# Attention stage: router products behind the fourth projection instead of the third, the last two turns behind the third instead of the second; first expert unit: its first low-weight pass behind the second tile's high passes

## The reference, cut to what matters

```python
h = _layernorm(x) * (1 + ca) + sa
qkva = einsum('bnd,ed->bne', rmsnorm(h), w_qkva)      # q, kv, a: 512 columns each
a = sigmoid(a);  s[t] = a[t] * s[t-1] + kv[t];  x = x + ga * q * s
h = _layernorm(x) * (1 + cb) + sb
probs = softmax(h @ Wr);  top 2 of 8 experts, capacity 160 rows for each sequence and expert
y = relu(h_e @ W1[e] + b1[e]) @ W2[e] + b2[e];  x = x + gb * (weighted sum of the two)
```

## Time and profile before

| | us |
|---|---|
| median of 3 runs | 2142.61 (2138.87 to 2143.8) |
| the profiled execution, its own time | 2142.84 |
| its span, first to last instruction | 2141.1 |
| TensorE busy | 2117.1 (99%) |
| VectorE busy | 1783.2 (83%) |
| ScalarE busy | 1062.6 (50%) |
| GpSimd busy | 368.9 (17%) |

### The profile page before, as it was taken

One profiled execution on the slowest core, in us unless ns is written; L12 is line 12 of the kernel. 1 busy time (PEld: TensorE's weight loads), 2 busy tenths in 40 slices (PEclk: granted clock), 3 DMA queues, 4 the chain that ended last, 5 costly groups with the idle time before them and its releaser, 6 DMA issues.

```text
span 2141.1 us, 35829 instructions
## 1 busy us (share of the span) xinstructions
PE 2117.1 (99%) x13366; PEld 1263.1 (59%) x13366; DVE 1783.2 (83%) x3040; ACT 1062.6 (50%) x2103; POOL 368.9 (17%) x337
## 2 busy tenths in 40 slices
PE   8999999999999999999999999999999999999998
PEld 3455444445474657656764765576466657656676
DVE  6899999999887887887888779778877887887754
ACT  5566666667372645355253625534461644356250
POOL 1134343433423010100001010101101010100101
PEclk9999999999999999999999999999999999999999
DMA  8899996876775641553265345416434551543212
GB/s 292 251 263 253 250 259 156 207 174 147 165 226 129 182 123 50 153 143 99 35 212 122 77 123 152 120 26 194 104 98 102 170 123 50 164 132 99 37 14 26
DMA packets 355390, 305.27 MB, mean 143 GB/s; under 512 B 242603, under 2 KB 242859, under 8 KB 354704
## 3 DMA queue, kind: packets, MB, share of 16 engines
q1 hardware_dynamic: 333312, 260.83, 44.2%
q0 software_dynamic: 21904, 42.14, 10.3%
HBM read 168.03 MB, written 93.01 MB: 122 GB/s over the span
## 4 chain that ended last, share of the span: by engine, by line
PE 93%; DVE 3%; DMA 1%; SPq 1%; issue 1%; ACT 1%; POOLq 0%; DVEq 0%; ACTq 0%
PE bank L2238 32%; PE bank L2146 21%; PE bank L2321 17%; PE bank L2331 9%; PE bank L2358 5%; PE bank L2349 4%; PE bank L2226 2%; PE bank L2092 1%; DMA reg_e<-reg_e 1%; SPq L592 1%; PE bank L2049 1%; DVE reg_a L1782 0%; DVE reg_e L1288 0%; PE bank L2293 0%; PE bank L2103 0%
## 5 line engine op out<-in xcount | busy, mean ns | idle before, releaser
L2146 PE MATMUL bank<-reg_c 128*128 128x512 f16 x2296 | 506.5, 380 | 0.0
L2238 PE MATMUL bank<-reg_e,reg_a 128*128 128x320 f16 x2880 | 447.5, 299 | 0.0
L2321 PE MATMUL bank<-reg_b,reg_c 128*128 128x512 f16 x1872 | 406.7, 379 | 0.2 <-DVE reg_e L1671 0.2
L2146 PEld LDWEIGHTS bank<-reg_c 128*128 128x128 f16 x2296 | 222.5, 98 | 258.7 <-issue 2.5
L2238 PEld LDWEIGHTS bank<-reg_e,reg_a 128*128 128x128 f16 x2880 | 280.9, 98 | 112.7
L2321 PEld LDWEIGHTS bank<-reg_b,reg_c 128*128 128x128 f16 x1872 | 182.8, 98 | 219.3 <-DVE reg_e L1671 2.3
L866 POOL DMA_INDIRECT out_dram<-reg_e,midx x79 | 138.8, 1756 | 951.0 <-DVE reg_e L1674 878.1
L2238 PE MATMUL bank<-reg_e,reg_d 128*128 128x320 f16 x1440 | 232.5, 299 | 0.0
L1089 ACT ACTIVATE reg_e<-bank,b1s 128x320 f32<-128x320 f32 x120 | 63.3, 527 | 252.8 <-PE bank L2238 252.6
L2238 PEld LDWEIGHTS bank<-reg_e,reg_d 128*128 128x128 f16 x1440 | 139.7, 98 | 57.6 <-ACT reg_e L1089 4.1
L807 POOL DMA_INDIRECT slot_rows<-reg_e,sli x112 | 126.2, 1127 | 101.0 <-DVE reg_e L1481 65.9
(11 more groups left out here) (278 smaller groups left out, 3406.9 us busy)
## 6 DMA issues: line engine op xcount, KB each, us to landing
reg_d<-in_w SPq DMA_DIRECT2D x232, 512.0 KB, 4.7
slot_rows<-zrow SPq DMA_DIRECT2D x32, 516.0 KB, 5.3
reg_b<-in_x SPq DMA_DIRECT2D x16, 1024.0 KB, 7.6
out_dram<-reg_b SPq DMA_DIRECT2D x16, 1024.0 KB, 8.9
reg_d<-in_w SPq DMA_DIRECT2D x8, 1024.0 KB, 9.6
reg_d<-in_wmod SPq DMA_DIRECT2D x5, 1024.0 KB, 11.1
slot_rows<-zrow SPq DMA_DIRECT2D x32, 129.0 KB, 5.2
reg_a<-in_w SPq DMA_DIRECT2D x8, 512.0 KB, 4.7
```

The source lines that it names most:

```text
L2146: ins = mm(dst[:, :], wqs[:, ws, kc, e0:e0 + P], xns[:, j % 2, xs, kc, :], start=kc == 0 and xs == 0 and ws == 0, stop=kc == KC - 1 and ws ...
L2238: ins = mm(dst[:, 0:CAP], w[ws][:, c, p * P:(p + 1) * P], xs_of[:, KC * xs + 2 * i + c, j * CAP:(j + 1) * CAP], start=first and c == 0 and ...
L2321: ins = mm(bank_y[i % 2][:, :], hid[:, hs, hc, t * P:(t + 1) * P], w2s[:, ws, hc, :], start=k == 0 and hs == 0 and ws == 0, stop=k == HC - ...
```

## The change

On TensorE the turns of tiles 2 and 3 move from behind k = 1 to behind k = 2, and the router products from behind k = 2 to behind k = 3, in every step. On VectorE `add_y` of tiles 2 and 3 moves behind `mix` of group 0. In unit 0 the high passes of tiles 0 and 1 come first, then the low passes of tile 0, the turns, the low passes of tile 1; the other tiles are as before. No instruction is added or taken away.

```diff
@@ VectorE, step
-                if has(i, -1):
-                    add_y(n - 1, pj, 2)
-                    add_y(n - 1, pj, 3)
                 if has(i, 0) and j == 0 and i > 0:
                     wait(dve, s_y, KC * n)
                     v_.tensor_copy(cga[:, :], gaS[:, :, q]).then_inc(s_cga, 1)
                     wait(dve, s_cga, 2 * q + 2)
                 if has(i, 0) and i > 0:
                     mix(q, j, 0)
+                if has(i, -1):
+                    add_y(n - 1, pj, 2)
+                    add_y(n - 1, pj, 3)
                 if has(i, -2):
                     route_choose(oq, oj)
@@ TensorE, step
-                    if k < 2 and has(i, -1):
-                        turn_y(q, j, 2 * k, i)
-                        turn_y(q, j, 2 * k + 1, i)
-                    if k == 2 and has(i, -2):
+                    if k in (0, 2) and has(i, -1):
+                        turn_y(q, j, k, i)
+                        turn_y(q, j, k + 1, i)
+                    if k == 3 and has(i, -2):
                         for t in range(TB):
                             logits(n - 2, oq, oj, t)
@@ TensorE, plain_unit (its matmuls now stand in hidden_tile, with the same waits)
+                high = tuple((kc, 0, xs) for kc in range(KC) for xs in range(2))
+                low = tuple((kc, 1, 0) for kc in range(KC))
+                mixed = tuple((kc, ws, xs) for kc in range(KC) for ws, xs in ((0, 0), (0, 1), (1, 0)))
+                hidden_tile(u, 0, high)
+                hidden_tile(u, 1, high)
+                hidden_tile(u, 0, low)
+                last_block(0)
+                hidden_tile(u, 1, low)
+                for hb in range(2, HC):
+                    hidden_tile(u, hb, mixed)
+                    last_block(hb)
```

More of the change, by code:

```diff
@@ L2208, in bank_free, with hidden_tile @@
                     pe.wait_ge(s_y, KC * NB - 1)
+            def hidden_tile(u, hb, passes):
+                for kc, ws, xs in passes:
+                    for b in range(2):
+                        i = 2 * hb + b
+                        if kc == 0 and ws == 0 and xs == 0:
+                            wait(pe, s_hhi, 2 * HC * u + i + 1)
+                            bank_free(i)
+                        if hb == 0 and ws == 1 and b == 0:
+                            wait(pe, s_wlo, kc + 1)
+                        ins = mm(bank_h[i % 4][:, 0:CAP], w1s[ws][:, kc, hb * P:(hb + 1) * P],
+                                 xT_of(u)[:, 4 * xs + kc, b * CAP:(b + 1) * CAP],
+                                 start=kc == 0 and ws == 0 and xs == 0, stop=kc == KC - 1 and ws == 1)
+                        if kc == KC - 1 and ws == 1:
+                            ins.then_inc(s_mm1, 1)
@@ L2210, in plain_unit @@
             def plain_unit(u):
                 pe.wait_ge(s_xt, 16 * (u + 1))
[L2213 to L2232, removed]
```

## The result

| | before | with the change |
|---|---|---|
| median of 6 runs, us | 2140.15 (2138.87 to 2143.8) | 2148.29 (2147.73 to 2150.31) |
| profiled execution: time, span, us | 2142.84, 2141.1 | 2148.09, 2146.3 |
| ratio to before | | 1.0036, 95% interval 1.0023 to 1.0049 |

The change makes the kernel about 0.36% slower, some 8 us. The two traces can explain the 5.25; the rest lies in executions of which there is no profile.

What follows compares the result with a forecast made beforehand. It took TensorE and VectorE as both near full, bound by a loop between them once router products move. Terms -1.2 - 5.5 - 0.7 + 10.9 = +3.5 us on 2142.84 gave 2146.3 us, range 2140.5 to 2150.8.

Steps and rivals of the forecast that it cites:

- The loop: Attention: router products release `route_choose`, VectorE's last y releases the next first turn; 34.34 or 35.54 us a step, 10.7 added.
- Its three parts: In the loop: T to `route_choose` 10.49 us, from there to the last y 23.65, last y to turn 0.20.
- the restarted turns: Attention, TensorE: turns restarted after a wait take some 0.04 us more, counted in the loop's 0.20.
- The gains of attention: Waits of TensorE removed: 1.2 us in step 1, together 5.5 us in steps 3, 7 and 11.
- The clock: Attention: no fall counted behind the new waits; 3 x 1.4 = 4.3 us kept for the range.
- Rival B: Attention: the loop closes and the clock falls after steps 5, 7 and 8; 2150.6 us, with one fall 2147.7; chance 0.27.
- The first unit: Unit 0, TensorE: last low passes start later, but with 16 matmuls, 2.2 us of work, already done; gain 0.7 us.
- T: Start of a step's first turn on TensorE, from which times are counted; an undisturbed step takes 33.75 us.
- the removed stall: Step 11, router products: 2.30 us of waiting for DMA transposes and 1.44 of slower clock would go.

Runs made afterwards that it cites:

- the repeat: The changed kernel run once more, unaltered, beside the kernel before on one chip: 1.0029 (1.0017 to 1.0042) of the kernel before.
- The run with the longer waits: The changed kernel with the router products another projection later, behind k = 4: 1.0254 (1.0233 to 1.0274) of the kernel before.
- the kernel with the turns in the gap: Kernel before, but in unit 0 the last block's turns stand between tile 0's high and low passes: 0.9990 (0.9980 to 1.0000) of before.
- the kernel with the turns alone: Kernel before with only the turns of tiles 2 and 3 and their `add_y` later, router products in their old place: 0.9999 (0.9990 to 1.0007).

## Why the prediction was right, and where it was not

**The loop** was right in place and size. Its three parts were forecast as 10.49, 23.65 and 0.20 us and measured 10.55, 23.69 and 0.06 in step 6. The prediction read 0.04 us for the restarted turns of step 1; its rows 4 give 0.20 (78.25 - 77.18 = 1.07 against 0.87), while in step 6 of the changed kernel they take 0.06 more (244.48 - 243.55 = 0.93), which is already in the 10.55. So this small term was near by luck, not by its reading. A step was forecast as 34.34 and 35.54; the thirteen steps from 2 to 14 measured 34.15 to 34.48, and 35.61, 36.22 and 35.31 in those with two maxima. The 36.22 is step 7, whose router products still waited 0.64 us for transposes. The prediction had that wait gone, and put one of 0.2 in step 11, where there was none. Moving one line closes the loop, one projection more lengthens the step by one projection, and moving `route_choose` opens it: shown by runs.

**The gains of attention** were right in the sum: step 1 gained 1.2 us (34.00 to 32.82), the 3.8 us at the router products went down to 0.8, and the clock did not fall in step 11. The stage came out at +4.25 against +4.2. That it fits to 0.05 us is luck: against the second profile of the kernel before the same stage is +3.1.

**The clock.** No fall behind the waits of 1.63, 1.45 and 1.33 us, neither here nor in the repeat: the granted clock is 1.00 in the 4 us behind each. Rival B did not come. With waits of 2.8 us and more in nearly every step the clock did fall, to 0.58 in the window above.
The Trainium skill (TensorE: Matmul & The Clock Gate, section "A second HAM failure mode: psum-queue depth-cycling") tells of a kernel in which short and frequent idling makes the clock swing between its levels. The twelve short waits of the changed kernel did not do that. The run with the longer waits does not test it, since single waits of 2.16 and 2.30 us were followed by a fall too.

**The first unit** is the step that failed. I wrote "Gain 0.7 us", and it was a loss of 1.65, or of 0.4 against the second profile of the kernel before; there is a gain against neither. The times up to the turns were right (last low passes at T + 37.2 forecast, turns at T + 37.63). What was wrong was to count the 16 high passes of tile 1 as 2.2 us of work saved. They had been the cover of ScalarE's activations, which start at the end of the turns. Moved ahead of them, they leave TensorE 8 matmuls, 1.1 us, to do before it needs a bank from ScalarE, and the 2.2 us come back as waits: the turns came 1.69 us later, and the 53.2 us from there to the second layer stayed. I had not followed ScalarE's program there: it waits for all turns before its first activation. The runs with the turns earlier and later show this chain.

**The size.** The forecast was 2146.3 us, the median 2148.29. As a change it was off by more: +3.5 forecast, +8.1 between the medians of six runs, +6.2 in the repeat. I took the profiled execution, 2142.84 us, for the time of the kernel before (median of three runs 2142.61); six runs gave 2140.15. An anchor that lay 2.7 us too high made up for part of a change that was forecast too small, and to that extent the nearness of 2146.3 is luck. The profile's difference of 5.25 us against +3.5 is the unit's 2.35, less the 0.6 us by which this execution reached step 1 sooner. The wait in step 11 varies from execution to execution, so the removed stall may have been smaller in the unprofiled ones than in the trace that I read. That this makes up the other 2.9 us is argued, not shown; the cause of that part stays open.

## What to carry to other kernels

Before an instruction is moved later on a busy engine, follow who waits for it, and from there round to the first wait of the same engine on that one: the sum of the pieces (to the release, the other engine's work, the way back) is the least length of a step, however full or empty either engine looks. Where the later place is wanted for a late transfer, move the consumer on the other engine by the same time. Work that is moved ahead of a wait may have been the cover of another engine's work behind it; read that engine's program too before the work is counted as gained.

## What was not expected of the hardware

Over the fourteen profiles TensorE's clock fell in the attention stage or unit 0 behind waits of 1.98 us (the kernel with the turns in the gap, step 11), 2.16 and 2.30 us and most of those near 3, and not behind 1.63 or 1.55. But the length of one wait does not settle it. In the kernel with the turns alone the clock fell in step 11 behind a wait of only 1.45 us:

```profile
422.20 0.24 PE L2103 MATMUL bank<-wrs,reg_e 128*128 128x16 f16 x4 [1.45 <-DMA reg_e<-reg_e]
...
423.00:427.00 4.00, 4.00 (x17) 1.51 (x14) 3.34 (x16) 2.69 (x6) 0.00 (x0) 0.57 1.05 389
```

And in the kernel with the router products behind k = 4 it held behind waits of 2.19, 2.77, 2.78 and 2.92 us; here the last of them, at the first turn of step 15:

```profile
604.63 1.09 PE L2092 MATMUL bank<-ident,reg_e 128*128 128x128 f32 x8 [2.92 <-issue]
...
604.00:608.00 4.00, 3.37 (x20) 2.06 (x21) 4.00 (x7) 0.00 (x0) 1.71 (x2) 1.00 1.14 227
```

What else decides it stays open.
